# A gated cross-attention and mixture-of-experts block: the setup before the attention loop reordered, causal masks moved off TensorE, and four products of zeros put on TensorE while the loads land

## What is computed

```
x = x + tanh(g_xattn) * attention(layernorm(x), ctx, ctx)      # 16 heads of 8 dims, causal mask k <= q
x = x + tanh(g_ffn)   * moe(layernorm(x))                      # 8 experts, top 2, capacity 160 of 1024 rows
moe: softmax(x @ Wr), top 2, rank in the expert, rows past the capacity dropped,
     h = gelu(x @ W1[e] + b1[e]), y = h @ W2[e] + b2[e], weighted sum of the two
```

## Time and profile before

| what | value |
|---|---|
| median of 3 runs | 172.25 us |
| profiled execution | 173.76 us, span 172.0 us |
| busy: TensorE, VectorE, GpSimd, ScalarE | 113.2, 101.6, 82.3, 68.5 us |
| setup, until the loop's first maximum starts | 29.42 us |
| loop, until its last packed sums (L754) | about 86 us |
| routing and experts | about 86 to 172 us |

### The profile page before, as it was taken

The page is one execution under the profiler, slowest core; times in us unless marked ns, Lnnn a source line. Parts: engine busy times, 40 slices in busy tenths (PEclk is TensorE's granted clock), DMA queues, the critical chain, the costliest instruction groups (busy, mean ns, idle before and its releaser), DMA issues.

```text
span 172.0 us, 2105 instructions
## 1 busy us (share of the span) xinstructions
PE 113.2 (66%) x655; PEld 79.6 (46%) x658; DVE 101.6 (59%) x264; ACT 68.5 (40%) x127; POOL 82.3 (48%) x117
## 2 busy tenths in 40 slices
PE   0375699989999998959644400079999999840000
PEld 0143466445555555625233300058999999730000
DVE  4989543575675654756377695026697776911044
ACT  2136322526644645716125420026655547410032
POOL 6878899998000000020587378200047775777400
PEclk9999999999999999999996555556999999997555
DMA  4997700340000000000198010266000111011083
GB/s 128 257 228 193 224 0 0 124 122 4 0 0 0 0 4 0 2 0 4 22 313 256 24 63 31 60 148 138 0 10 8 33 34 37 27 39 32 26 258 108
DMA packets 19193, 12.72 MB, mean 74 GB/s; under 512 B 2440, under 2 KB 17623, under 8 KB 19184
## 3 DMA queue, kind: packets, MB, share of 16 engines
q1 hardware_dynamic: 17616, 10.37, 22.8%
q0 software_dynamic: 1280, 2.10, 3.8%
q10 hardware_dynamic: 288, 0.13, 0.3%
HBM read 7.57 MB, written 5.32 MB: 75 GB/s over the span
## 4 chain that ended last, share of the span: by engine, by line
PE 35%; DVE 18%; issue 17%; POOL 16%; DMA 8%; POOLq 1%; another core or an unknown queue 1%; SPq 1%; ACT 0%; DVEq 0%
POOL results L479 8%; PE turn L683 7%; POOL slots L469 6%; PE sc L899 4%; DVE top L982 4%; PE av L740 3%; DVE xn_all L975 3%; PE turn L696 3%; DMA xn_all<-results 2%; DMA X<-x 2%; PE av L746 2%; PE turn L884 2%; PE sc L715 2%; PE turn L702 2%; DVE stats L962 1%
## 5 line engine op out<-in xcount | busy, mean ns | idle before, releaser
L479 POOL DMA_INDIRECT results<-p,result_of x24 | 25.5, 1062 | 27.2 <-DVE p L1147 18.4
L982 DVE TENSOR_REDUCE top<-turn 128x3 fp32r<-128x462 f32 (+2 forms) x44 | 26.0, 605 | 19.2 <-PE turn L683 9.5
L469 POOL DMA_INDIRECT slots<-rows,slot_of x16 | 16.9, 1059 | 14.9 <-DVE slot_of L1056 10.8
L683 PE MATMUL turn<-shared,q_all 128*128 128x462 f32 (+2 forms) x44 | 22.0, 517 | 1.8 <-DVE top L982 0.9
L374 POOL TENSOR_TENSOR rstd<-mean_var,half 128x4 f32<-128x4 f32 (+1 forms) x5 | 4.6, 918 | 33.4 <-DVE mean_var L968 33.4
L562 ACT ACTIVATE p_all<-sc 128x1024 f32<-128x1024 f32 x16 | 15.5, 1021 | 10.5 <-PE sc L718 9.5
L899 PE MATMUL sc<-q_all,w_all 128*128 128x320 f32 x96 | 17.7, 338 | 0.2 <-issue 0.2
L606 ACT ACTIVATE p_all<-sc,B 128x320 f32<-128x320 f32 x32 | 14.7, 527 | 3.5 <-PE sc L899 3.2
L899 PEld LDWEIGHTS sc<-q_all,w_all 128*128 128x128 f32 x96 | 15.6, 207 | 0.8 <-issue 0.3
L884 PE MATMUL turn<-identf,parts_all 128*128 128x128 f32 (+1 forms) x24 | 5.8, 325 | 13.7 <-DMA parts_all<-slots 13.7
L683 PEld LDWEIGHTS turn<-shared,q_all 128*128 128x128 f32 x44 | 9.2, 211 | 10.5 <-ACT q_pack_all L535 4.7
(11 more groups left out here) (168 smaller groups left out, 247.3 us busy)
## 6 DMA issues: line engine op xcount, KB each, us to landing
W<-w SPq DMA_DIRECT2D x8, 256.0 KB, 3.3
p_all<-w SPq DMA_DIRECT2D x8, 256.0 KB
slots<-slot SPq DMA_DIRECT2D x1, 1320.0 KB, 9.8
parts_all<-slots SPq DMA_DIRECT2D x8, 132.0 KB, 2.4
results<-zeros SPq DMA_DIRECT2D x1, 1024.0 KB, 11.2
xn_all<-results SPq DMA_DIRECT2D x4, 256.0 KB, 3.6
X<-x SPq DMA_DIRECT2D x2, 256.0 KB, 3.5
out<-X SPq DMA_DIRECT2D x4, 128.0 KB, 1.8
```

The lines of the kernel that those rows point to most:

```text
L469: nc.gpsimd.indirect_dma_start(out=slots, out_offset=bass.IndirectOffsetOnAxis(ap=slot_of[:, c:c + 1], axis=0), in_=rows[:, c // TOPK, :], ...
L479: nc.gpsimd.indirect_dma_start(out=results, out_offset=bass.IndirectOffsetOnAxis(ap=result_of[0:m, e, n:n + 1], axis=0), in_=y[0:m, e % 2, ...
L683: mm = pe.matmul(o, qT[:, 0, b, qt * P:qt * P + P], kTr[:, b, h0:h0 + nh, 0:keys], start=True, stop=(qt >= 2), skip_group_check=True)
L982: dve.tensor_reduce(top[:, qt, h0:h0 + nh, 3 * HD], ps[:, 0:nh * keys].rearrange("p (h k) -> p h k", h=nh), AX.X, ALU.max).then_inc(turn_f ...
```

## The change

The setup is put in another order, and some of its work moves to other engines.

- VectorE takes the statistics of both batches before the first layernorm; it no longer clears v0, v1 and top. ScalarE clears them with copies of `zeros` (1024, 1024 and 2048 columns) ahead of its first copy out of PSUM (semaphore `zeroed`).
- GpSimd takes the root of both batches in a row, writes the selections straight into pack_k and pack_q (ScalarE's two copies L503 go), then makes the copies in CT and keys_for_max of batch 0, and only then the ones and masks.
- TensorE runs four products of zeros (512, 512 and 256 columns ahead of the keys, 256 behind them) into a PSUM bank that nobody reads; pack_keys 1 to 3 go between the first maxima; turn_rows(1) follows the fifth maximum instead of preceding the first; queries(1) goes to the bank sc1.
- The four mask products of each scores(g) go, with mask_k0. GpSimd instead sets the exponentials of later keys to zero after the exponential (`later_keys`, 512 columns for each g), and values(g - 1) waits for it (`masked`). The splits of the weights go between them, two parts for each of g = 0 to 3.
- Waits for k_ready and the second queries move from before the loop to before the first last_scores.

```diff
@@ -143,8 +142,9 @@
         parts_all = sb("parts_all", [P, 2 * 2 * 4 * S], F16)
-        pack_raw = parts_all[:, 0:2 * 2 * 2 * 4 * P].bitcast(F32).rearrange(
-      "p (k w i j s d) -> p k w i j s d", k=2, w=2, i=4, j=4, s=4)
+        pack_k_raw = q_pack_all[:, 0:2 * 4 * P].bitcast(F32).rearrange(
+      "p (w i j s d) -> p w i j s d", w=2, i=4, j=4, s=4)
+        pack_q_raw = pack_q[:, :, :, :, :, :].bitcast(F32)
@@ -381,17 +382,27 @@
       root((0, QT), 1)
+      root((QT, NT), 2)
+      pool.wait_ge(cleared, 1)
+      packing(pack_k, [kp for kp, qp in PRODUCTS]).then_inc(pack_ready, 1)
+      packing(pack_q, [qp for kp, qp in PRODUCTS]).then_inc(pack_ready, 1)
...
-      pool.wait_ge(cleared, 1)
-      packing(pack_raw[:, 0], [kp for kp, qp in PRODUCTS]).then_inc(pack_raw_ready, 1)
-      packing(pack_raw[:, 1], [qp for kp, qp in PRODUCTS]).then_inc(pack_raw_ready, 1)
-      root((QT, NT), 2)
-      pool.wait_ge(cleared, 2)
+      def keys_for_max(b, h0):
+          pool.tensor_tensor(kTr[:, b, h0:H],
+                             kT_part[:, 0, b, 0:C].unsqueeze(1).to_broadcast([P, H - h0, C]),
+                             head_mask[:, :, :].rearrange("p i j -> p (i j)")[:, h0:H].unsqueeze(2)
+                             .to_broadcast([P, H - h0, C]), ALU.mult).then_inc(kTr_ready, 1)
+      pool.wait_ge(kT_split, 1)
+      keys_for_max(0, FIRST_HEADS)
+      pool.wait_ge(zeroed, 1)
       step(pool.memset(v0[:, :, :, HD:HD + 1], 1.0))
@@ -402,20 +413,7 @@
-      def keys_for_max(b, h0):
-          pool.tensor_tensor(kTr[:, b, h0:H],
-                             kT_part[:, 0, b, 0:C].unsqueeze(1).to_broadcast([P, H - h0, C]),
-                             head_mask[:, :, :].rearrange("p i j -> p (i j)")[:, h0:H].unsqueeze(2)
-                             .to_broadcast([P, H - h0, C]), ALU.mult).then_inc(kTr_ready, 1)
-      pool.wait_ge(kT_split, 1)
-      keys_for_max(0, FIRST_HEADS)
-      pool.memset(mask_k1[:, :], 0.0)
-      step(pool.memset(mask_k0[:, :], 0.0))
-      pool.affine_select(out=mask_k0[:, :], in_=mask_k0[:, :], compare_op=ALU.is_ge, fill=NEG,
-                         base=0, pattern=[[1, P]], channel_multiplier=-1)
+      step(pool.memset(mask_k1[:, :], 0.0))
       for j in range(4):
@@ -454,9 +452,20 @@
-      for n in range(2 * SPLIT_FIRST):
-          split_weights(n)
-      root(blocks[0], 3)
+      def later_keys(g):
+          pool.wait_ge(sc_free, 3 * g + 2)
+          m = p0[:, g % 2, :, 0:P]
+          pool.affine_select(out=m, in_=m, compare_op=ALU.is_ge, fill=0.0, base=0,
+                             pattern=[[0, 4], [1, P]], channel_multiplier=-1).then_inc(masked, 1)
+      for g in range(NG):
+          if g == 7:
+              root(blocks[0], 3)
+          later_keys(g)
+          if g < SPLIT_FIRST:
+              split_weights(2 * g)
+              split_weights(2 * g + 1)
@@ -486,6 +495,17 @@
       act.dma_start(WQ[:, :], wqT).then_inc(wq_in, 16)
+      def clear(dst, n):
+          return act.activation(dst, zeros[:, :].unsqueeze(1).to_broadcast([P, n, D]), ACT.Copy)
+      act.wait_ge(zero_ready, 1)
+      for v in (v0, v1):
+          last = clear(v[:, :, :, :].rearrange("p b h d -> p (b h d)") if v is v0 else
+                       v[:, :, :, :, :].rearrange("p b i j d -> p (b i j d)"), B * H * VW // D)
+      last.then_inc(zeroed, 1)
+      clear(top[:, :, :, :].rearrange("p t h d -> p (t h d)"), QT * H * 4 * HD // D).then_inc(zeroed, 1)
       act.wait_ge(kv_ps, 1)
@@ -495,15 +515,9 @@
           act.wait_ge(q_ps, b + 1)
-          act.activation(qT[:, 0, b, :], sc[:, 2 + b, :], ACT.Copy).then_inc(q_high, 1)
-      def packing(n):
-          act.wait_ge(pack_raw_ready, n + 1)
-          act.activation((pack_k, pack_q)[n][:, :, :, :, :, :], pack_raw[:, n], ACT.Copy).then_inc(pack_ready, 1)
+          act.activation(qT[:, 0, b, :], (sc[:, 2, :], sc1[:, :])[b], ACT.Copy).then_inc(q_high, 1)
       turned_rows(0)
-      packing(0)
       high_queries(0)
@@ -638,13 +651,25 @@
+      def fill(n):
+          pe.matmul(sc[:, 3, 0:n * P], zeros[:, :], zeros[:, :].unsqueeze(1).to_broadcast([P, n, D]),
+                    start=True, stop=True, skip_group_check=True)
+      pe.wait_ge(zero_ready, 1)
+      for n in (4, 4, 2):
+          fill(n)
...
+      fill(2)
       def queries(b):
           pe.wait_ge(xnT_ready, b + 1)
-          pe.matmul(sc[:, 2 + b, :], WQ[:, :], xnT[:, b, :], start=True, stop=True).then_inc(q_ps, 1)
+          if b:
+              pe.wait_ge(k_packed, 3)
+          pe.matmul((sc[:, 2, :], sc1[:, :])[b], WQ[:, :], xnT[:, b, :], start=True,
+                    stop=True).then_inc(q_ps, 1)
@@ -660,7 +685,9 @@
       pe.wait_ge(pack_ready, 1)
-      for i in range(4):
+      def pack_keys(i):
           if i >= 2:
@@ -712,10 +739,7 @@
               q = slice(32 * j, 32 * j + 32)
-              pe.matmul(sc[:, j, :], k_pack[q, i, b, 0:P], q_pack[q, i, b, :], start=True, stop=False,
-                        skip_group_check=True)
-          for j in range(4):
-              mm = pe.matmul(sc[:, j, 0:P], identb[:, :], mask_k0[:, :], start=False, stop=True,
+              mm = pe.matmul(sc[:, j, :], k_pack[q, i, b, 0:P], q_pack[q, i, b, :], start=True, stop=True,
                              skip_group_check=True)
@@ -736,6 +760,7 @@
           pe.wait_ge(sc_free, 3 * g + 3)
+          pe.wait_ge(masked, g + 1)
           for j in range(4):
@@ -820,20 +845,26 @@
-      turn_rows(1)
+      pack_keys(0)
...
-      maxima(maxima_first[:3])
+      maxima(maxima_first[0:2])
+      pack_keys(1)
+      maxima(maxima_first[2:3])
+      pack_keys(2)
+      maxima(maxima_first[3:4])
+      pack_keys(3)
+      maxima(maxima_first[4:5])
+      turn_rows(1)
+      maxima(maxima_first[5:6])
       project_values()
-      maxima(maxima_first[3:])
+      maxima(maxima_first[6:])
...
-      pe.wait_ge(k_ready, 1)
       pe.wait_ge(consts3, 1)
-      pe.wait_ge(q_ready, 2)
       for g in range(NG + 2):
@@ -843,6 +874,9 @@
           maxima(maxima_beside(g, 1))
+          if g == 0:
+              pe.wait_ge(k_ready, 1)
+              pe.wait_ge(q_ready, 2)
           if g < NG:
@@ -1057,11 +1091,12 @@
-      dve.memset(pack_raw[:, :, :, :, :, :, :], 0.0).then_inc(cleared, 1)
+      dve.memset(pack_k_raw, 0.0)
+      dve.memset(pack_q_raw, 0.0).then_inc(cleared, 1)
       dve.wait_ge(x_in[0], 16)
       statistics((0, QT), X)
-      dve.memset(v0[:, :, :, :], 0.0)
-      dve.memset(v1[:, :, :, :, :], 0.0).then_inc(cleared, 1)
+      dve.wait_ge(x_in[1], 16)
+      statistics((QT, NT), X)
       layernorm((0, QT), X, xn, xn_ready)
@@ -1073,18 +1108,15 @@
                         .to_broadcast([P, FIRST_HEADS, C]), ALU.mult).then_inc(kTr_first, 1)
-      dve.wait_ge(x_in[1], 16)
-      statistics((QT, NT), X)
-      dve.memset(top[:, :, :, :].bitcast(F32), 0.0).then_inc(cleared, 1)
...
-          dve.tensor_tensor(qT[:, 1, b, :], sc[:, 2 + b, :], qT[:, 0, b, :],
+          dve.tensor_tensor(qT[:, 1, b, :], (sc[:, 2, :], sc1[:, :])[b], qT[:, 0, b, :],
                             ALU.subtract).then_inc(q_ready, 1)
       low_queries(0)
-      dve.wait_ge(cleared, 3)
+      dve.wait_ge(zeroed, 2)
...
```

More of the change, by code:

```diff
@@ L107, in build @@
         mask_q = sb("mask_q", [P, 4, P], BF16)
-        mask_k0 = sb("mask_k0", [P, P], BF16)
         mask_k1 = sb("mask_k1", [P, 32], BF16)
@@ L222, in build @@
         turn_full, turn_free = sem("turn_full"), sem("turn_free")
-        pack_raw_ready, pack_ready = sem("pack_raw_ready"), sem("pack_ready")
+        pack_ready = sem("pack_ready")
         sc_full, sc_free, pv_done = sem("sc_full"), sem("sc_free"), sem("pv_done")
+        masked = sem("masked")
         oT_ready = sem("oT_ready")
@@ L227, in build @@
         upto_cleared = sem("upto_cleared")
-        cleared = sem("cleared")
+        cleared, zeroed = sem("cleared"), sem("zeroed")
         gate_ready = sem("gate_ready")
@@ L517, in place_values @@
                 act.wait_ge(kv_ps, 2)
-                act.wait_ge(cleared, 2)
+                act.wait_ge(zeroed, 1)
                 act.activation(v0[:, :, :, 0:HD],
@@ L527, in _ @@
             turned_rows(1)
-            packing(1)
             place_values()
```

## The result

The changed kernel took 165.87 us (median of 4 runs, 165.67 to 166.02), the kernel before 172.07 (171.27 to 177.01, four runs): ratio 0.965 with a 95% interval of 0.962 to 0.969. That is 6.2 us less, faster as forecast, but 9.3 were expected. Two later comparisons of the same two kernels on other occasions, six runs of the changed one each, gave 0.950 (0.942 to 0.959) and 0.967 (0.959 to 0.976).

A forecast was written before the change was run, and what follows sets the result against it. It took the setup's chain of waits and TensorE's lower clock to bound the loop's start, then TensorE the loop. Terms 7.7 + 0.4 + 1.4 = 9.5 off 172.25 gave 162.8, about 163 us; range 160.3 to 168.8.

The forecast's parts named there:

- The setup: Before the loop: new order and upper clock start the loop at 21.7 instead of 29.42 us, -7.7.
- the sum: Whole kernel: 7.7 before the loop, 0.4 from its first products, 1.4 from mask products, together 9.5 us.
- The fillers: Products of zeros at TensorE's start: cost 0, at most 0.5 us, and buy the upper clock before the loop.
- the half-clock rival: Before the loop: clock stays at or falls back to the lower level, loop at 27.4, 168.9 us; chance 0.18.
- The rule on transposes: Between fillers and maxima: four transpositions, not counting as activity like products, might take the higher clock level away.
- The masks: Rounds 0 to 6: dropping mask products saves 0.2 us each on TensorE, -1.4; bounds 0 and 2.8.
- the bound of 2.2: GpSimd's later_keys in the loop: clearing 512 columns takes 2.2 us at most; cost to the kernel 0.
- move with their start: Stages after the loop: chains of latencies through DRAM that shift with their start.
- The rival in which the clock falls inside the loop: Rounds 0 to 6: less activity lowers the clock, 20 us slower, at 183; chance 0.03.
- the same offset: Whole run: profiled time before lies 1.5 us above the median, so 164.3 becomes a median of 162.8.
- the forecast's own case: Whole kernel: expected course with no rival coming true, 160.3 to 164 us; chance 0.60.
- a rival that was not in the sum: Setup: second layernorm or constants meet GpSimd, loop 1.7 us later, 164.5, up to 165.6; chance 0.14.

The follow-up runs named there:

- gap_fill: Changed kernel plus two products of zeros in TensorE's rest before round 6's normalised rows: 161.26 us, ratio to before 0.941.
- no_fill: Changed kernel without its four products of zeros: 165.84 us, ratio to before 0.963.
- fill_only: Kernel before with the four products of zeros added and nothing else: 174.29 us, ratio to before 0.988.
- quad_gap: Changed kernel plus two products of zeros in round 6, rerun on the last chip: 162.87 us, ratio to before 0.948.
- masks_back: Changed kernel with the mask products on TensorE again and GpSimd's clearing removed: 162.97 us, ratio to before 0.948.
- the pair on one chip: Changed kernel plus two products of zeros in round 6, with masks on TensorE (164.63 us) or on GpSimd (162.87 us).
- quad_masks: Changed kernel with mask products on TensorE again, no products in round 6, rerun on the last chip: 165.29 us, ratio to before 0.955.
- setup_fill: Changed kernel with more products of zeros in the setup, behind the keys and between turn_rows(0) and queries(0): 164.20 us.

## Why the prediction was right and where it missed

**The setup** was right in size, 8.5 us against 7.7, and partly by luck. What stood ahead of the first maxima had been read rightly: turn_rows(1) in front, top and the second statistics on VectorE, and the collision with GpSimd. The path to it was not the one foretold. The clock was to stay up from the start; it was down from 9 to about 16 us, and the first maximum came 1.7 us late. This was made up behind it. From the first maximum to queries(1) the sum had 7.1 us (4.4 of work, 1.1, 0.6 and a wait of 1.0 for VectorE), and 5.45 passed (13.72 to 19.17 in the timeline); from there to the loop it had 2.6, and 1.7 passed. Where the clock held (gap_fill), the first maximum started at 12.14 (12.0 foretold) and the loop at 18.74 (21.7), and TensorE waited 0.23 us for VectorE. GpSimd's constants were done at 18.8, not at 20.0 to 21.2, since the selections took 3.3 us as in their row and the copies in CT 0.47 instead of 1.24.

**The fillers** were to buy the clock. In no_fill the loop starts as early without them, and in fill_only they bring the start of the loop forward by 0.07 us. What the setup gained in these profiles is the order's doing. That the half-clock rival was set at 168.9 came from the same belief, that without fillers the clock stays low up to the loop. That the fillers never help is not shown: with them, some executions kept the clock through 9 us and started the loop 2.1 us earlier, and the one profile without them did not.

**The rule on transposes** (the Trainium skill, "TensorE: Matmul & The Clock Gate", Part 4: a transposition does not count as the engine being busy the way a product does) pointed at the right place. In the changed kernel the clock fell around the first turn_rows(0), 9.09 to 10.2, behind a rest of 2.1 us, and again around the turned rows at 66.11, behind one of 1.9. But neither is enough by itself at the late place: quad_gap has the same four transpositions without the rest and no fall, masks_back has both (the rest 1.98) and no fall. Whether transpositions count for less than products, no run here shows.

**The masks** were worth 1.4 in the sum. At a held clock the profiles give 0.94 over the rounds; the pair on one chip gives 0.8 to 1.8 in all, not clear of its noise, and some of it belongs to the constants that the loop waits for when mask_k0 is built. From loop start to residual the changed kernel took 40.64 us against 42.00: 1.4 less, with 1.8 expected, the masks and the loop's first low products. GpSimd's clearing took 0.64 us for 512 columns, under the bound of 2.2, and nothing waited for it.

**The step that failed** is the sentence that the later stages "move with their start". By the residual the gain was 9.9; 2.9 went back between 66 and 78 us. The rival in which the clock falls inside the loop named the mechanism, but I placed it in rounds 0 to 6, at 20 us and 0.03, and never asked about the last rounds, where TensorE rests 1.9 us for the normalised rows. The kernel before had the same rest (1.88 us, 74.1 to 75.99) and kept its clock there in the profile. Closing the rest gives 3.4 us back, which is shown. That taking the masks away is part of why the clock falls there is borne out by the profiles, five with the fall against four without, but how it does so is not shown. Nor are mask products a guarantee: runs of quad_masks were at 0.79 and 0.82, and of the kernel before at 0.78 (183.40 us); none of these has a profile.

**The base.** The profile of before (173.76) was 1.7 us above the median of its runs, that of after at its own. I took the same offset for both. In the spans the gain was 8.2, of which 1.3 appears only in the last 30 us: the last scatter of results starts at 160.3 in before's profile and at 152.0 in after's, 8.3 apart, where up to the eleventh, at 142.1 before, the two had stayed 7.1 apart. In the profiled executions 7.8 us stand against the sum's 9.5: 1.7 is the change's miss. The rest of the gap between 9.3 and 6.2, 1.4, is this offset.

The range held the time; the forecast's own case, 160.3 to 164, did not. It was reached by kernels with the clock held, not by the changed one. Two slips of the sums changed nothing: the lower end of 160.3 counts masks at 2.8 and no handovers, which give 160.8, and the absence of a rival that was not in the sum; and the chances above the range add up to 0.17, not 0.15.

## What to carry to other kernels

When a change makes TensorE's neighbours faster or takes work off TensorE, look through the whole program for places where it rests among light work, and not only at the stage that is edited: here 2.9 of 9.9 us gained were lost 45 us later. Products on zeros are cheap there if they end before the wait does and write to a bank that is about to be overwritten. Where equal shapes have two durations in one profile, take several profiles of one program before a cause is named, sort them by the fall itself and not by a mean over the run, and compare medians on one chip.

## What was not expected of the hardware

- One program had different courses of TensorE's clock: the same setup fell to the lower level at 9 us in one execution (queries(0) 2.08 us, loop at 20.88) and kept the upper one in another (1.12 us, 18.74). The changed kernel's four first runs agreed within 0.35 us at a mean clock of 0.83, and its later twelve went from 164.7 to 170.0.
- The granted clock's record is 1.00 until its first entry, whatever the products take: before's entry comes at about 30 us, and products up to there take 0.75 us for 462 columns and 0.46 after; no_fill's comes at about 15, and its row reads 1.00 from 9 to 16 us, where the changed kernel's reads 0.51 over the same products.
- Products of zeros raise the clock as others do: in the changed kernel six records of fillers from 1.52 us on, and then the keys in 0.72 us where they took 1.44. When it rises varies: in fill_only the keys took 1.05, in setup_fill 1.28.
- A profiled run's time is longer than its span by 2.0 to 2.2 us in the nine with masks on GpSimd, and by 1.76 to 1.78 in the five with masks on TensorE. The 0.35 us or so came with the step that moved the masks to GpSimd, and count against it in every comparison of times; why is open.
